# An attention and expert kernel: GpSimd instead of VectorE multiplies the scaled h by out_w

## The reference

```
h = jnp.einsum('bhst,bhtd->bhsd', C / (normalizer + EPS), vh)
mean = h.mean(-1, keepdims=True)
var = ((h - mean) ** 2).mean(-1, keepdims=True)
hn = (h - mean) / jnp.sqrt(var + LN_EPS)
hn = hn * out_w.reshape(nh, dh)[None, :, None, :]
...
x = x + _L0_xattn_ref(_layernorm(x, axis=-1), ctx_1024, ctx_1024, ...)
x = x + _L0_ffn_ref(_layernorm(x, axis=-1), ...)
```

## Time and profile before

| what | value |
|---|---|
| median of the runs | 648.44 us |
| time of the profiled execution | 651.1 us |
| its span, first to last instruction | 649.1 us |
| TensorE busy | 611.4 us (94%) |
| VectorE busy | 487.2 us (75%), 1330 instructions |
| ScalarE busy | 323.4 us (50%) |
| GpSimd busy | 193.7 us (30%), 185 instructions |
| mean granted TensorE clock | 0.986 |

### The profile page before, as it was taken

How to read it: one execution, slowest core, us unless ns; L and a number is a source line. 1 busy time by engine, 2 the same in 40 slices (tenths; PEclk the granted TensorE clock), 3 DMA queues, 4 the chain that set the end, 5 groups by cost and what they waited for, 6 DMA issues and landing times. The chain is left out here.

```text
span 649.1 us, 20273 instructions
## 1 busy us (share of the span) xinstructions
PE 611.4 (94%) x6736; PEld 526.6 (81%) x6737; DVE 487.2 (75%) x1330; ACT 323.4 (50%) x767; POOL 193.7 (30%) x185
## 2 busy tenths in 40 slices
PE   1799999999999899999999999999999999999995
PEld 1567777777777668998988988888989888989994
DVE  2546988999999898995888967666676757575684
ACT  2677888897988747544432323233232323232341
POOL 3000002242433424235345523232222323232333
PEclk9898998999999999999999999999999999999998
DMA  4443635475655626233464432323132323243510
GB/s 143 134 127 118 209 99 187 147 238 194 220 166 142 198 91 231 70 73 92 75 186 108 70 68 38 65 36 65 33 62 33 66 33 66 67 119 81 141 34 2
DMA packets 56044, 70.22 MB, mean 108 GB/s; under 512 B 5584, under 2 KB 50832, under 8 KB 55840
## 3 DMA queue, kind: packets, MB, share of 16 engines
q1 hardware_dynamic: 42560, 51.80, 26.3%
q0 software_dynamic: 13296, 17.32, 14.7%
q10 hardware_dynamic: 112, 0.08, 0.0%
HBM read 41.50 MB, written 24.92 MB: 102 GB/s over the span
## 5 line engine op out<-in xcount | busy, mean ns | idle before, releaser
L1059 ACT ACTIVATE decay_slots<-scores,b_turned 128x256 f32<-128x256 f32 (+1 forms) x312 | 124.4, 451 | 241.2 <-PE scores L1545 235.1
L1545 PE MATMUL scores<-x_slots,w_halves 128*128 128x256 f16 (+1 forms) x1760 | 193.7, 266 | 0.0
L1545 PEld LDWEIGHTS scores<-x_slots,w_halves 128*128 x1760 | 165.2, 98 | 17.3
L662 POOL DMA_INDIRECT expert_rows<-xf_rows,slot_i x64 | 71.9, 1124 | 211.8 <-issue 107.0
L1559 PE MATMUL pv<-w_halves,decay_slots 128*128 x864 | 97.6, 273 | 0.0
L684 POOL DMA_INDIRECT out_rows<-v_centred_and_one,row_ids x36 | 58.3, 1619 | 129.2 <-DVE v_centred_and_one L2146 95.7
L1559 PE MATMUL gate_bank<-w_halves,q_and_k_halves 128*128 x840 | 95.0, 273 | 0.0
L1559 PEld LDWEIGHTS pv<-w_halves,decay_slots 128*128 128x128 f16 x864 | 84.4, 98 | 9.7
L1559 PEld LDWEIGHTS gate_bank<-w_halves,q_and_k_halves 128*128 128x128 f16 x840 | 82.0, 98 | 9.5
L684 POOL DMA_INDIRECT out_rows<-work,row_ids x35 | 56.2, 1605 | 104.6 <-DVE work L2146 82.6
L1278 PEld LDWEIGHTS pv<-v_centred_and_one,decay_slots 128*128 128x128 f32 x512 | 63.7, 194 | 1.6
(11 more groups left out here) (263 smaller groups left out, 864.5 us busy)
## 6 DMA issues: line engine op xcount, KB each, us to landing
weight_stage<-in_L_ffn_w SPq DMA_DIRECT2D x32, 512.0 KB, 4.0
x_slots<-in_x SPq DMA_DIRECT2D x16, 512.0 KB, 4.4
weight_stage<-expert_rows SPq DMA_DIRECT2D x30, 272.0 KB, 3.2
ctx_slots<-in_ctx SPq DMA_DIRECT2D x8, 512.0 KB, 6.0
out_rows<-x_slots SPq DMA_DIRECT2D x8, 512.0 KB
v_centred_and_one<-expert_rows SPq DMA_DIRECT2D x9, 272.0 KB, 3.0
expert_rows<-v_centred_and_one SPq DMA_DIRECT2D x9, 272.0 KB, 3.2
xf_rows<-w_halves SPq DMA_DIRECT2D x4, 512.0 KB, 4.1
```

Source lines behind the costliest of these rows:

```text
L662: pool.indirect_dma_start(table, bass.IndirectOffsetOnAxis(ap=sloti[:, step[1], j, k:k + 1], axis=0), xfn[:, step[1], j, :], None, bounds_ ...
L1059: ins = act.activation(hf[:, f * R:f * R + tr.rows(0)], ps_s[:, q, n * R:n * R + tr.rows(0)], ACT.Gelu, bias=b1T[:, bass.ds(expert, 1), f] ...
L1545: ins = pe.matmul(o, w, xh[:, tr.slot(0) % 2, b, k, 0:tr.rows(0)], start=(n == 0), stop=(n == 3 * KC - 1))
```

## The change

For steps 0 to 6 the product with out_w is taken from VectorE's list and put into GpSimd's. Step 7 keeps it on VectorE. On GpSimd it stands, for steps 0 and 1, ahead of the first scatter, and for steps 2 to 6 between the seventh and the eighth scatter of the step two before. It waits for the scaled h (s_ho) there; x1_of waits for it through s_hw as before. In first_steps x1_of of step 1 goes behind c_of(S2, 0) and choose(S0).

```diff
+                def h_weighted(step):
+                    pool.wait_ge(s_ho, number(step) + 1)
+                    pool.sem_inc(s_held, 1)
+                    pool.tensor_tensor(work[:, :, :], work[:, :, :],
+                                       outw[:, :].unsqueeze(1).broadcast_to([P, SB, D]), ALU.mult).then_inc(s_hw, 1)
+
-                def scatter(step):
+                def scatter(step, beside=None):
...
                     for j in range(SB):
                         for k in range(2):
+                            if j == SB - 1 and k == 1 and beside is not None:
+                                h_weighted(beside)
                             if j:
                                 pool.wait_ge(s_sc[step[1]][k], step[0] * SCATTERED + j * 16)
...
                 def body(last, step, nxt, after):
                     if last is not None:
-                        scatter(last)
+                        scatter(last, None if nxt == LAST else nxt)
 
                 def first_steps():
-                    scatter(S0)
+                    h_weighted(S0)
+                    h_weighted(S1)
+                    scatter(S0, S2)
...
                         h_scaled(step)
-                        h_weighted(step)
                     if last is not None:
                         choose(last)
...
                     h_scaled(S0)
-                    h_weighted(S0)
                     c_of(S1, 0)
...
                     h_scaled(S1)
-                    h_weighted(S1)
-                    x1_of(S1)
                     c_of(S2, 0)
                     choose(S0)
+                    x1_of(S1)
```

## The result

The changed kernel took 664.24 us (median of four executions, 660.92 to 668.95) against 648.68 us before: ratio 1.0246, 95% interval [1.0168, 1.0323]. Measured again beside the last experiments it was 665.85 against 651.31, 1.0247 [1.0203, 1.0291]. It is slower by 2.5%, where the prediction said half a per cent and its range ended at 656.0. The ratios here are those of the comparison on one chip; they need not be the quotients of the medians.

The account below looks back on a forecast made before the run. VectorE was taken as a bound, TensorE close behind. Steps 2 to 5 at +0.71 us each (+2.84), step 6 +0.3 and step 0 +0.1 gave +3.2 us, 651.6 us on the median; range 647.3 to 656.0.

Parts of the forecast that it names:

- the limit by the scores: Second c_of on VectorE needs TensorE's second scores, so a step can gain 0.18 us, not 1.14.
- The full gain: Rival: TensorE's scores come earlier along with VectorE, six steps gain up to 1.14 us each, 641.6 us; chance 0.08.
- the length of the product: GpSimd's product with out_w takes 2.3 us, with 4.6 us as the upper end.
- the hold: Steps 2 to 5: GpSimd's product blocks choose's eighth operation on VectorE for 1.85 us, a net +0.71 us a step.
- the 0.2 us of the cast: Lower bound of the hold: a VectorE cast took 0.63 us instead of 0.42 while GpSimd issued a transfer.
- Choose starts at 147.02: Step 3 on VectorE: with the product gone, choose starts at 147.02 us instead of 148.16.
- Step 6: GpSimd is free only after choose is over, so nothing is blocked; x1_of starts later, +0.3 us.
- the clock falls: Rival: longer TensorE waits in steady steps lower its clock; 654.8 us with two of four steps, 658.0 with all; chance 0.17.
- the fall of step 2: Old profile, 108 to 112 us: clock 0.71 and 0.50 after a 1.21 us TensorE wait, 1.6 us of full speed lost.

Follow-up runs that it names:

- the run of steps 2 to 6: Against the kernel before, only the products of steps 2 to 6 moved to GpSimd, steps 0 and 1 left as they were; 662.32 us, ratio 1.0205.
- the run with c_of and gate_bias inside choose: Against the changed kernel, next step's first c_of, then gate_bias, put between choose's second and third operations; 655.42 us, ratio 1.0077 to the kernel before.
- the run without the products and with the order fitted: Against the changed kernel, products of steps 0 to 6 left out and weights_low put ahead of x1_of; 648.91 us, ratio 0.9971 to the kernel before.

## Why the prediction was wrong

**Right: the limit by the scores.** It said 0.18 us a step where the products go; without them the steps from 3 on gained 0.1 to 0.2, and the second c_of waited 0.15 us for its scores. The full gain is out.

**Right: the length of the product.** 2.35 to 2.40 us, forecast 2.3. The Trainium skill (GPSIMD Engine Reference, Performance versus the Vector engine) led to an estimate of 2.25, which the trace bears out within 0.12 us.

**Right in kind, too small: the hold.** The operation waits to the end of the product, not for the 0.2 us of the cast. The Trainium skill (SBUF — State Buffer, Who interferes with whom) says that the second to issue is blocked until the first has finished; the ends agree (product to 153.39, operation to 153.45; product to 177.95, operation to 178.00), and the c_of with an input in PSUM is not held, as the page has it. The recorded starts do not always bear out that order: some held operations start ahead of the product (229.93 against 230.56 above). It was the third operation and not the eighth, because of a wait that the prediction did not have: choose cannot start when the product is gone, since the router's product on TensorE ends only 1.7 us after the scaled h starts. Before, the product of 1.14 us stood in that slot. "Choose starts at 147.02" was therefore wrong by 0.5 us, and a hold ranges from 1.3 to 2.3 us instead of 1.85. In the prediction's own terms a long one makes -1.14 + 0.50 + 2.17 = +1.53 us a step, and the steps 3 and 4 of the run of steps 2 to 6 grew by 1.5 at full clock, forecast 0.71. In the changed kernel's steady steps at full clock it was 0.76 and 1.07. Step 6, where no hold was forecast, was held too (0.78 more instead of 0.3), because GpSimd was free before the scaled h there: the product began at 244.80 us, the third operation at 244.97. All holds and waits together are 5 to 9 us by the reckonings above, forecast 3.2.

**Wrong: the clock.** The step that failed is the rival "the clock falls", in its chance (0.17) and in its price (1.6 us a fall). The sum itself put the clock at nothing. The rival named what happened, more waiting of TensorE and a lower clock, and with two of four steps in the first profile (3 and 5) even the number, which is luck: the second profile has one such fall and a short one. But its price was read from the fall of step 2, of 3.5 us, and these were 14 us at 0.51 to 0.53. Against the same steps of the run of steps 2 to 6, with the same holds at full clock (28.88 and 27.47 us), they cost 4.5 and 5.4 us of time. And the chance was too low because the prediction followed the lost time only along VectorE. It wrote that the step grows by 0.71, and of TensorE's waits only that they might take 0.7 more; it never asked who waits for the first c_of. TensorE's second scores do, and the waits of 0.2 to 1.2 us there came on top of the two that it already had the earlier trace rows, themselves longer in some steps (0.74 and 1.32 instead of 0.40 and 1.04). That these new waits brought the falls is not shown, as the count above says; that the clock was lower is (0.961 to 0.984 in the ten executions, 0.978 to 0.994 in the 65 of before). The Trainium skill (TensorE: Matmul & The Clock Gate, A second HAM failure mode: psum-queue depth-cycling) tells of a kernel whose TensorE idled briefly between groups of matmuls, often enough that its clock went to and fro between the two levels. The falls behind waits of 1.1 to 1.2 us are in line with that; the twin run, with the same waits and no fall, shows that it need not happen.

For the profiled execution the terms now add up. Holds and waits of steps 2 to 6 make 1.07 + 1.48 + 0.76 + 1.66 + 0.78 = 5.8 us, with the two steps that had a fall taken at full clock from the run of steps 2 to 6 (forecast 3.2); the two falls make 4.5 + 5.4 = 9.9 (forecast nothing); what comes before step 2, 2.1 (forecast 0.1), mostly the longer fall from step 1 to 2, which is not shown to be the change's. Together that is 17.8, and the span grew by 17.7.

## What to carry to other kernels

An operation that is taken off a full engine is worth only what the next consumer can use. Look for what it was covering: here it filled a slot in which VectorE would have waited for TensorE, and leaving it out altogether saved 0.2 to 0.3%, not clear of the noise. A two-input operation of GpSimd that reads SBUF, beside an operation of VectorE with two inputs in SBUF, cost VectorE the rest of GpSimd's instruction here; put work with an input in PSUM beside it, or count the hold in full. And when a change makes a nearly full TensorE wait longer, give a fall of its clock a place in the sum, and price it by what 10 to 15 us at half speed would cost in that stage, not by the shortest fall in the old profile.

## What the hardware showed that was not expected

- A one-input multiplication on GpSimd takes longer than a two-input one of the same size (2.77 to 2.83 against 2.35 to 2.40 us), and yet holds VectorE for less: in steps 3, 4 and 5 the held operation ended 1.12 to 1.14 us after the start of an instruction of 2.8 us, where the two-input one held to its end.
- The clock does not answer to the same waits in the same way. Two executions with the same wait of 1.05 to 1.07 us in step 3 stayed at 1.00 in one and fell to 0.5 for 14 us in the other, and ten executions of the changed kernel range from 0.961 to 0.984.
- A hold can be longer than the product. In five of the profiled steps the held operation of VectorE starts 0.07 to 0.65 us ahead of GpSimd's product in the record, while a scatter ahead of the product runs, and all five end 0.05 to 0.06 us behind the product; the longest took 3.08 us. Beside a scatter alone such operations took 0.19 us (at 233.25 and 233.47 us of the run with c_of and gate_bias inside choose).
- The clock fell for 10 us without any new wait, in the run without the products and with the order fitted (from 188 us on).
